# Four key tiles of values in one visit, denominators behind them, and a ring of 16 probability tiles

## The reference

```
xn = layernorm(x)
q, k, v = (xn @ W_qkv) in 16 heads of 64
scores  = q @ k.T / 8
weights = softmax(scores)
s = (weights @ v) @ W_out
g = silu(top-2-of-8 expert FFN(xn) + shared FFN(xn))
x = x + s * g
... layer 1: a convolution over time and a gated FFN with 4-bit weights, the same x + s * g
```

## Time and profile before

| | |
|---|---|
| device time, median of 2 runs (2219.2 to 2220.79) | 2219.99 us |
| span of the profiled execution, first to last instruction | 2261.7 us |
| PE busy | 2007.7 us (89%) |
| DVE busy | 1718.4 us (76%) |
| POOL busy | 1615.8 us (71%) |
| ACT busy | 1121.3 us (50%) |
| mean granted clock of PE | 0.954 |

### The profile page before, as it was taken

One profiled execution on the slowest core, in us unless ns is written; L12 is line 12 of the kernel. 1 busy time (PEld: TensorE's weight loads), 2 busy tenths in 40 slices (PEclk: granted clock), 3 DMA queues, 4 the chain that ended last, 5 costly groups with the idle time before them and its releaser, 6 DMA issues. The chain is left out here.

```text
span 2261.7 us, 33617 instructions
## 1 busy us (share of the span) xinstructions
PE 2007.7 (89%) x8183; PEld 1155.2 (51%) x8183; DVE 1718.4 (76%) x2770; ACT 1121.3 (50%) x2031; POOL 1615.8 (71%) x1394
## 2 busy tenths in 40 slices
PE   5799999999999999999999999999996997454676
PEld 4355555555555555555555555555554665242354
DVE  7777777777777777777777777777776997258996
ACT  1355554555555545555555455555555886142533
POOL 4277777777777777777777777777776996714785
PEclk9899999999999999999999999999998999675889
DMA  5101000111010001110100011101003442101000
GB/s 192 34 22 26 22 21 21 26 27 25 21 26 22 21 21 26 27 26 21 26 22 21 21 25 27 26 21 26 22 21 111 138 142 76 50 14 49 0 14 23
DMA packets 70435, 84.75 MB, mean 37 GB/s; under 512 B 9272, under 2 KB 47480, under 8 KB 69760
## 3 DMA queue, kind: packets, MB, share of 16 engines
q1 hardware_dynamic: 50176, 57.08, 10.4%
q0 software_dynamic: 7552, 20.98, 2.8%
q10 hardware_dynamic: 12672, 6.29, 0.9%
HBM read 30.84 MB, written 18.87 MB: 22 GB/s over the span
## 5 line engine op out<-in xcount | busy, mean ns | idle before, releaser
L1085 POOL TENSOR_TENSOR psum_k<-psum_k,probs 128x512 f32<-128x512 f32 x768 | 959.6, 1279 | 80.5 <-ACT probs L1047 77.1
L1047 ACT ACTIVATE probs<-ps_s 128x512 f32<-128x512 f32 x1024 | 593.4, 597 | 732.8 <-PE ps_s L986 686.7
L1102 DVE TENSOR_REDUCE mxh<-ps_m 128x1 f32<-128x512 f32 x1044 | 683.7, 681 | 275.8 <-PE ps_m L940 262.4
L949 PE MATMUL ps_v<-probs,V 128*64 128x512 f32 x2048 | 488.8, 603 | 0.0
L985 PE MATMUL ps_s<-Q,K 128*128 128x512 f32 x1024 | 460.5, 450 | 0.0
L940 PE MATMUL ps_m<-K,Q 128*128 128x512 f32 x1044 | 420.4, 404 | 31.0 <-DVE mxh L1102 30.3
L986 PE MATMUL ps_s<-Q,K 72*128 72x512 f32 x1024 | 406.5, 397 | 0.0
L1085 POOL TENSOR_TENSOR psum_k<-probs 128x512 f32<-128x512 f32 x128 | 160.8, 1276 | 301.9 <-ACT probs L1047 301.9
L985 PEld LDWEIGHTS ps_s<-Q,K 128*128 128x128 f32 x1024 | 192.7, 188 | 300.8 <-issue 197.2
L949 PEld LDWEIGHTS ps_v<-probs,V 128*64 128x64 f32 x2048 | 127.0, 136 | 246.5 <-issue 156.9
L940 PEld LDWEIGHTS ps_m<-K,Q 128*128 128x128 f32 x1044 | 199.7, 191 | 100.4 <-DVE mxh L1102 53.3
(11 more groups left out here) (251 smaller groups left out, 2669.2 us busy)
## 6 DMA issues: line engine op xcount, KB each, us to landing
K<-K SPq DMA_DIRECT2D x132, 128.0 KB
Q<-Q SPq DMA_DIRECT2D x132, 128.0 KB, 2.4
rows<-zeros SPq DMA_DIRECT2D x4, 1536.0 KB, 15.1
r_x_raw<-rows SPq DMA_DIRECT2D x24, 256.0 KB, 3.4
results<-r_y_row ACTq DMA_DIRECT2D x24, 256.0 KB, 2.3
x_tok<-in_X SPq DMA_DIRECT2D x4, 512.0 KB, 5.5
x<-in_X SPq DMA_DIRECT2D x4, 512.0 KB, 5.2
out_x<-out_t SPq DMA_DIRECT2D x8, 256.0 KB, 2.3
```

Source lines behind the costliest of these rows:

```text
L949: nc.tensor.matmul(ps_v[hf][rows, :], V[par][:, kt, rows], probs[:, k % NPR, :], start=kt == 0, stop=kt == KT - 1).then_inc(pv_done, 1)
L1047: nc.scalar.activation(probs[:, k % NPR, :], ps_s[x][:, :], ACT.Exp, scale=SCALE).then_inc(p_done, 1)
L1085: nc.gpsimd.tensor_tensor(acc, probs[:, (k - 2) % NPR, :] if kt == 1 else acc, probs[:, k % NPR, :], ALU.add).then_inc(add_done, 1)
L1102: nc.vector.tensor_reduce(mxh[:, i % 8, i // 8:i // 8 + 1], ps_m[i % 2][:, :], AX.X, ALU.max).then_inc(m_done, 1)
```

## The change

The values of the four latest tiles are made in one visit, at steps 5, 9 and 13, and those of the last four tiles of a pair at step 1 of the next pair. The denominators move from steps 2 and 10 to steps 1 and 9 and stand behind the values there. The ring of probabilities grows from 8 slots (4 tiles of two heads) to 16, and ACT's wait for PE's use of a slot goes, since PE's own order covers it. The mask shrinks to its distinct numbers and is broadcast. `V[1]` is set to zero ahead of the loop, because the first pair now also has a visit for a pair that doesn't exist; the last pair has its last visit behind the loop.

```diff
-NPR = 8
-ADD0 = 8
+NPR = 16
+ADD0 = 16
...
+    GROUP = 4
+    RING = NPR // 2
+    P0 = 2
...
-    LIST = [("K0", 0, "v"), ("K1", 1, "v"), ("den1", 2, "v"), ("Q0", 3, "v"), ("max1", 6, "v"), ("out1", 7, "v"),
-            ("Q1", 8, "v"), ("V0", 9, "a"), ("den0", 10, "v"), ("V1", 11, "a"), ("VT0", 13, "a"), ("max0", 14, "v"),
+    LIST = [("K0", 0, "v"), ("K1", 1, "v"), ("den1", 1, "v"), ("Q0", 3, "v"), ("max1", 6, "v"), ("out1", 7, "v"),
+            ("Q1", 8, "v"), ("V0", 9, "a"), ("den0", 9, "v"), ("V1", 11, "a"), ("VT0", 13, "a"), ("max0", 14, "v"),
...
-                        if t:
-                            pe.wait_ge(p_done, n * CK + 2 * t + x - 1)
+                        pe.wait_ge(p_done, P0 + n * CK + 2 * t + x - 1)
...
                     for name in STEP[t]:
-                        other(n, par, name, b)
-                    if t >= 3 and t % 2:
-                        values(n, par, t - 3)
-                        values(n, par, t - 2)
-                values(n, par, STEPS - 2)
-                values(n, par, STEPS - 1)
+                        if name[:3] != "den":
+                            other(n, par, name, b)
+                    if t == 1:
+                        for k in range(STEPS - GROUP, STEPS):
+                            values(n - 1, 1 - par, k, False)
+                    elif t % GROUP == 1:
+                        for k in range(t - 1 - GROUP, t - 1):
+                            values(n, par, k)
+                    for name in STEP[t]:
+                        if name[:3] == "den":
+                            other(n, par, name, b)
+            for k in range(STEPS - GROUP, STEPS):
+                values(N - 1, 1, k)
...
-                            if t >= 4:
-                                act.wait_ge(add_done, ADD0 + n * 2 * ADDS + added(t - 4))
-                                act.wait_ge(pv_done, n * CK + 2 * (t - 4) + 2)
+                            if t >= RING:
+                                act.wait_ge(add_done, ADD0 + n * 2 * ADDS + added(t - RING))
                             else:
-                                act.wait_ge(add_done, ADD0 + n * 2 * ADDS + added(t + STEPS - 4) - 2 * ADDS)
+                                act.wait_ge(add_done, ADD0 + n * 2 * ADDS + added(t + STEPS - RING) - 2 * ADDS)
...
+            nc.gpsimd.memset(V[1][:, :, :], 0.0).then_inc(preset, 1)
...
-                            mask[DH:K2R, x, :].rearrange("p (j q) -> p j q", j=4), ALU.mult)
+                            mask[DH:K2R, x, :].unsqueeze(2).to_broadcast([NM, 4, P]), ALU.mult)
```

More of the change, by code:

```diff
@@ L46, in attention_early @@
     g.psum_k = [[sb(f"psum_k{h}{x}", [P, CH], F32) for x in range(2)] for h in range(2)]
-    g.mask = sb("mask", [K2R, 2, CH], F32)
+    g.mask = sb("mask", [K2R, 2, 4], F32)
     g.ones = sb("ones", [P, DH], F32)
@@ L941, in half_row, with values @@
                                  start=True, stop=True).then_inc(m_ready, 1)
-            def values(n, par, t):
+            def values(n, par, t, unseen=True):
                 hf, kt = divmod(t, KT)
@@ L946, in values @@
                     k = 2 * t + x
-                    pe.wait_ge(p_done, n * CK + k + 1)
+                    if unseen:
+                        pe.wait_ge(p_done, P0 + n * CK + k + 1)
                     rows = slice(x * DH, (x + 1) * DH)
@@ L965, in _ @@
             for x in range(2):
-                nc.tensor.matmul(ps_v[1][x * DH:(x + 1) * DH, :], ones[:, :], probs[:, x, :], start=True, stop=True)
+                nc.tensor.matmul(ps_v[1][x * DH:(x + 1) * DH, :], ones[:, :], probs[:, x, :], start=True, stop=False)
+            pe.wait_ge(preset, 4)
             for n, par in pairs(pe):
@@ L1030, in _ @@
             nc.scalar.activation(warm[:, :], ones[:, 0:1], ACT.Exp)
+            act.sem_inc(p_done, P0)
             for name in FIRST:
@@ L1079, in _ @@
                             k = 2 * t + x
-                            pool.wait_ge(p_done, n * CK + k + 1)
+                            pool.wait_ge(p_done, P0 + n * CK + k + 1)
                             if kt > 1:
@@ L1879, in layouts @@
     carry[:, :, 0] = 0.0
-    mask = np.zeros((2, 8, 4, P), np.float32)
+    mask = np.zeros((2, 8, 4), np.float32)
     for x in range(2):
@@ L1897, in layouts @@
         "wout_d": c(a["L0_attn_W_out"].reshape(PAIRS, P, D).transpose(1, 0, 2)),
-        "mask_d": c(mask.transpose(1, 0, 2, 3).reshape(8, 2, CH)),
+        "mask_d": c(mask.transpose(1, 0, 2)),
         "dt_d": c(np.tile(a["L1_attn_dt"], 2).reshape(P, 1)),
```

## The result

The changed kernel takes 2295.3 us (2293.93 and 2296.67) against 2219.99 us before: ratio 1.0333, 95% interval 1.0316 to 1.035. It is slower, as forecast, but by 75 us instead of 49, and 4 us above the range. The profiled execution has a span of 2292.1 us.

The account below looks back on a forecast made before the run. The loop is bound by PE's instruction stream. Per pair 1.87 + 2.13 - 1.52 - 1.06 = +1.42 us, times 32 = +45.4; extra visit +3.6, last denominator -0.3: 2220.0 + 48.7 = 2269 us, range 2238 to 2291.

Parts of the forecast that it names:

- What bounds the kernel: Attention loop: bound by PE's instruction stream, busy 98.41 of 100 us; DVE saturated in steps 1 to 6, resting later.
- Switches removed, 1.52 us: Visits and denominators on PE: fewer switches into and out of them, 2.79 us a pair before, 1.27 after.
- that rival: Denominator behind a visit keeps its own switch: +0.68 us a pair, 22 us in all, 2291 us; chance 8%.
- the switches alone: Rival: DVE's chain in the bare stretches doesn't reach PE, so only the gains count: 2141 us; chance 9%.
- The wait at step 2, 1.06 us: PE's product for the maximum at step 2 starts 0.96 us late, its successor 0.10; the visit ahead removes both.
- Two stretches without cover, 1.87 and 2.13 us: Between visits, steps 2 to 5 and 10 to 13: PE needs 5.05 us, DVE's chain 6.82 and 7.08; PE waits.
- T: Start of the first product for the maximum of step 2; step 5's was forecast 6.82 us later.
- the rival of faster reductions: DVE's reductions at their least time in both bare chains: 0.7 us a pair, 22 us in all, 2246; chance 14%.
- PE's steps 6 to 8 and 14 to 1 have the projections; there PE leads as now: Behind the visits at 5 and 13 DVE has only `attn`, `max` and `out`; no new wait was counted there.
- A longer ring frees nobody: ACT's wait on the ring ends when scores alone would release it, 0.56 us behind L986; edit priced at nothing.
- The clearing falls on POOL where it waits 39.10 us: Ahead of the loop: larger clearing of `probs` and that of `V[1]` fall in POOL's waiting time; priced at nothing.
- The clock: Rival: PE's clock falls to 1.2 GHz behind waits in steps 5 and 13, +3.4 us twice a pair, some 2480; 2%.

Follow-up runs that it names:

- the two kernels: Changed kernel with Q0, V1, VectorE's list and clearing moved: period 48.00, ratio 0.9692; kernel before with 16 slots and VectorE's K0, K1 a step later: 49.54, 0.9909.
- one quarter of the reciprocals: Changed kernel with three of the four quarters of each denominator's reciprocal left out on VectorE: 2253.34 us, ratio 1.0147.
- the denominators back: Changed kernel with the denominators back at steps 2 and 10, visits of four tiles kept: 2275.03 us, ratio 1.0243.
- both lists fitted: Changed kernel with TensorE's Q0, V1 and VT0 one step later, VectorE's list made for it, and only 2 slots cleared early: 2201.52 us, ratio 0.9692.

## Why the prediction was right or wrong

**What bounds the kernel: right.** PE's stream sets the loop as long as DVE keeps within one step of it, and DVE's free time (24%) was in the wrong steps. Moving DVE's work alone was worth 2.34 us a pair.

**Switches removed, 1.52 us: right in its parts.** The visit with the denominator behind it takes 4.45 us, as worked out, so the denominator has no switch of its own, and that rival is out. No run has the switches alone; 48.00 against 49.54 us fits, though the two kernels differ in more.

**The wait at step 2, 1.06 us: right.** It is gone in the trace after.

**Two stretches without cover, 1.87 and 2.13 us: right.** From T to the L943 behind it pass 6.84 and 6.92 us against 6.82 and 7.08, so 1.89 and 1.97 us. The 0.16 us that the second chain is shorter are two reductions in a row in 1.13 instead of 1.22 us and PE's start 0.68 instead of 0.75 us behind that of the last reduction. That is all that came of the rival of faster reductions, which had 0.35 in either chain.

**"PE's steps 6 to 8 and 14 to 1 have the projections; there PE leads as now": wrong.** The visit behind step 15 had been cover for `max0` and `out0` on DVE. Without it PE starts 0.36 us late in step 0 (0.18 of idle time in the row, released by a reduction) and pays 0.10 for it: 0.46 us, 15 us in all.

**"A longer ring frees nobody": wrong, the other way.** The longer ring and ACT's shorter wait are worth 0.22 us a pair, 7 us in all. With both, 1.97 + 1.89 + 0.46 - 1.52 - 1.06 - 0.22 = 1.52 us against 1.54 measured and 1.42 forecast. The sum for the period was good to 4 us of the 49.

**"The clearing falls on POOL where it waits 39.10 us": wrong for one of the two.** That of `V[1]` does. That of `probs` stands in an earlier stage, beside DVE's normalisation, and I didn't look at DVE's rows there: 3607 ns at most with a clearing of 3.54 us was already in the trace of before. The start is 4.0 us later, 3.5 of them already behind the normalisation. The run with late clearing shows the cause: with 14 of the 16 slots cleared later, the kernel is 9 us faster. The Trainium skill, SBUF — State Buffer, section SBUF: two separate sides, says that GpSimd and a VectorE operation that uses both of its ports take a shared pair of ports as an exclusive lock for a whole instruction. The traces agree with such a lock: 7.02 us against 6.96 of the clearing, 3.61 against 3.54, 2.79 against 2.65 and 1.05 against 0.98. That this operation uses both of its ports no row shows.

**The clock: the failed term.** The sum put it at nothing. It was a rival with 2%, on the ground that it stays at 1.00 through the wait of 0.79 us, and priced as if it fell behind every wait, over 200 us. In the changed kernel it falls behind the wait of 1.15 us, in every third pair, for 3.4 us at a time and 1.55 us of loss. That is 17 us of the 27 that were missing; without it the time would lie inside the range. What the prediction cites from the Trainium skill (TensorE: Matmul & The Clock Gate, section Part 1: The HAM clock gate), that idleness of PE halves its clock, the trace bears out: 0.50 behind that wait. What failed is the step from one wait that did no harm to pairs of waits, of that size and longer: with one quarter of the reciprocals, waits of 0.50 and 0.79 us are followed by a fall in 25 pairs. The prediction also set its 1.24 and 1.50 us, by which PE starts late, beside 0.79 us of idle time in a row; that row's start is 0.96 late. In idle time the new waits are 0.90 and 1.15 us.

So the forecast kept its sign and its mechanism; 27 us were missing: 17 of the clock, 4 of the start, 4 of the period, and 2 that I can't place.

**Left open.** What decides how often the clock falls. It isn't the idle time in a pair: the kernel with one quarter of the reciprocals has the shortest waits (0.50 and 0.79 us, 1.5 us apart) and the most falls, 25; that with the denominators back has nearly the same pair of waits (0.51 and 0.80) and 5. Their periods differ (49.79 and 51.51), but no run changed the period alone, so whether that is the reason isn't shown.

## What to carry to other kernels

Before work of one engine is gathered into fewer, larger blocks, lay the other engines' queues beside the gaps that this opens: with a lead of one step allowed, the follower's work per stretch has to fit, not per pair, and a second list written by hand has to move with the first. The same grouping was 3.3% slower with VectorE's list as it stood and 3.1% faster with both lists fitted and the clearing moved (9 us, or 0.4%, by itself). And a stall of PE has to be priced with the clock that it may cost: here 17 us beside the 49 us of the longer period.

## What was not expected of the hardware

The granted clock fell to 0.50 behind idle gaps of PE of 0.9 to 1.2 us, each with a gap of 0.34 us some 2.8 us ahead of it, inside a loop in which PE is busy 94% of the time, and stayed there for some 3.4 us. With the lone gap of 0.79 us in the kernel before it never fell in the loop. The number of falls doesn't follow the length of the gaps: 25 with gaps of 0.50 and 0.79, 20 with 0.95 and 2.96.

An operation of 0.34 us on VectorE took 3.61, 7.02, 2.79 or 1.05 us, each time as long as what GpSimd was clearing beside it (3.54, 6.96, 2.65 and 0.98 us). In these places the time of a GpSimd memset was paid by VectorE, however idle GpSimd was.

With the ring of 16 and ScalarE's wait without the one for the values, the exponentials started 0.05 to 0.06 us earlier in nine of 16 steps, and a period of 50 us was 0.22 us shorter.
